# Delta-rule layer on one NeuronCore: six of its causal convolutions move from VectorE to TensorE, and the start is reordered

## The reference, cut to what matters

```python
def conv(x, w):                          # w has 4 taps, shared by all channels
    xp = pad(x, 3 rows of zeros in front)
    return w[0]*xp[:, 0:T] + w[1]*xp[:, 1:T+1] + w[2]*xp[:, 2:T+2] + w[3]*xp[:, 3:T+3]
q = silu(conv(x @ Wq, conv_q)); k = silu(conv(x @ Wk, conv_k)); v = silu(conv(x @ Wv, conv_v))
beta = sigmoid(x @ Wb); q, k = l2norm per head
A = (k*beta) @ k.T ; M = strict_lower(A) + I ; u = M^-1 (v*beta) ; w = M^-1 (k*beta)   # per chunk
# scan over the chunks: u -= w S ; o = q S + lower(q k.T) u ; S += k.T u
o -> per-head RMS norm * onorm_w -> @ Wo
```

## Time and profile before

| what | value |
|---|---|
| profiled execution, device time | 962.78 us |
| its span | 961.0 us (1.8 us lie around it) |
| runs, median | 962.0 us |
| PE, DVE, ACT busy | 86%, 69%, 38% of the span |
| bodies 0 to 8 and their tail | 0 to 702.5 us |
| routed experts and output | 702.5 to 961.0 us |

### The profile page before, as it was taken

One profiled execution on the slowest core, in us unless ns is written; L12 is line 12 of the kernel. 1 busy time (PEld: TensorE's weight loads), 2 busy tenths in 40 slices (PEclk: granted clock), 3 DMA queues, 4 the chain that ended last, 5 costly groups with the idle time before them and its releaser, 6 DMA issues. The chain is left out here.

```text
span 961.0 us, 30663 instructions
## 1 busy us (share of the span) xinstructions
PE 822.5 (86%) x13456; PEld 629.2 (65%) x13456; DVE 661.5 (69%) x1220; ACT 364.8 (38%) x683; POOL 116.7 (12%) x173
## 2 busy tenths in 40 slices
PE   6794779789999999999999787998779999999910
PEld 5683665676777777687687464666566887788800
DVE  2799699799789789879877988787691222222238
ACT  2605334435534644544554451332321222222215
POOL 2000000000000000000000000000002454544345
PEclk9895988999999999999999987998889999999965
DMA  8301004300101021020020020020176999999376
GB/s 307 72 23 47 3 3 168 108 3 25 62 18 39 3 69 27 24 70 23 4 69 24 3 70 23 2 89 2 48 286 220 362 362 346 344 360 358 96 266 278
DMA packets 49632, 113.09 MB, mean 118 GB/s; under 512 B 8688, under 2 KB 8816, under 8 KB 49504
## 3 DMA queue, kind: packets, MB, share of 16 engines
q1 hardware_dynamic: 44384, 100.70, 29.1%
q0 software_dynamic: 5120, 10.49, 4.8%
HBM read 84.34 MB, written 26.84 MB: 116 GB/s over the span
## 5 line engine op out<-in xcount | busy, mean ns | idle before, releaser
L468 PE MATMUL bank<-xnT,wring 128*128 128x256 f32 x768 | 183.6, 396 | 2.1 <-ACTq L681 1.3
L468 PEld LDWEIGHTS bank<-xnT,wring 128*128 128x128 f32 x768 | 149.3, 198 | 24.9 <-ACTq L681 1.5
L587 PE MATMUL bank<-late,ffn_w 128*128 128x256 f32 x480 | 117.3, 394 | 0.0
L1754 DVE TENSOR_TENSOR hid<-ps_g,sg 128x160 f32<-128x160 f32 x32 | 10.4, 324 | 148.5 <-ACT sg L1650 148.5
L942 DVE SCALAR_TENSOR_TENSOR cv<-pre,taps,cv 128x1024 f32<-128x1024 f32 x72 | 92.4, 1283 | 18.1 <-ACTq L707 14.4
L587 PEld LDWEIGHTS bank<-late,ffn_w 128*128 128x128 f32 x480 | 90.8, 195 | 15.2 <-issue 1.1
L1509 POOL MEMSET xgT<- 128x512 f32 x2 | 1.0, 532 | 686.9 <-POOLq L1834 686.9
L1609 PEld LDWEIGHTS ps_g<-xgT,wring 128*128 128x128 f32 x640 | 74.4, 192 | 10.9 <-issue 10.9
L1609 PE MATMUL ps_g<-xgT,wring 128*128 128x128 f32 x640 | 74.8, 275 | 1.3 <-ACT xgT L1640 1.3
L1640 ACT ACTIVATE xgT<-ps_x 128x320 f32<-128x320 f32 x32 | 14.0, 437 | 132.8 <-PE ps_x L1598 132.8
L549 PE MATMUL bank<-wo,o_ch 128*128 128x512 f32 x128 | 60.1, 605 | 0.6 <-DVE o_ch L1086 0.6
(11 more groups left out here) (202 smaller groups left out, 1474.2 us busy)
## 6 DMA issues: line engine op xcount, KB each, us to landing
wring<-in_ffn_W_gate SPq DMA_DIRECT2D x20, 512.0 KB, 7.6
wring<-in_ffn_W_up SPq DMA_DIRECT2D x20, 512.0 KB, 9.6
wring<-in_ffn_W_down SPq DMA_DIRECT2D x20, 512.0 KB, 10.7
x_in<-in_attn_x SPq DMA_DIRECT2D x8, 512.0 KB, 3.7
x_res<-in_attn_x SPq DMA_DIRECT2D x8, 512.0 KB, 4.8
side_rows<-late SPq DMA_DIRECT2D x8, 512.0 KB, 7.0
x_rows<-x SPq DMA_DIRECT2D x8, 512.0 KB, 3.2
h_rows<-h SPq DMA_DIRECT2D x8, 512.0 KB, 4.4
```

The source lines that it names most:

```text
L468: m = te.matmul(bank[:, c * COLS:(c + 1) * COLS], wqkv[:, w, kt, ct * P:(ct + 1) * P], xnT[:, kt, :], start=(kt == 0), stop=(kt == KT - 1))
L587: m = te.matmul(bank[:, c * COLS:(c + 1) * COLS], w[:, kt, ft * P:(ft + 1) * P], hT[:, kt, :], start=(kt == 0), stop=(kt == KT - 1))
```

## The change

Six convolutions are made by matmuls: of k in bodies 1 and 7, of v in bodies 0, 1, 2 and 7. ACT builds 8 matrices of 128 x 128 (the identity times one tap) at the start. For each half (4 of the 8 tiles, 512 columns) PE adds four matmuls, one for each tap, over shifted views of `pre`. The filler letters are C (k) and D (v), each 4 pieces of 2 matmuls and 2 banks. ACT takes the first exponential, and DVE the product, straight from these banks; the bank is released by DVE. DVE's three taps and ACT's second copy go.

In body 0 the k and q convolutions stay on DVE but run in halves; ACT's order is changed so that silu of k starts after three projections; silu and turn of v move ahead of `problems`; the scaling of `wo` goes from DVE's end of body 0 to ACT; the layernorm of step 2 (`first_norm(2)`, X, `take_x(2)`) goes from body 0 and the head of body 1 into the middle of body 1, and one semaphore of the halos becomes three. In bodies 1, 2 and 7 DVE does silu and turn of v right behind residual(1), and ACT takes silu of v behind take_output(0), ahead of the old step's rstd.

```diff
+CONV_K = (1, STEPS - 1)
+CONV_V = (0, 1, 2, STEPS - 1)
-FILLS = {0: ["BGGGGXPPPPPPPPPPPP"],
+FILLS = {0: ["BGGGGDDDDXPPPPPPPPPPPP"],
+         1: ["BCC", "CCD", "DDD", "X", "GPPPP", "G", "G", "G", "PP", "PP", "PP", "", "", "PP", "", "O"],
+         2: ["BXWW", "WWWD", "WWWD", "DDPP", "GPP", "G", "G", "G", "PP", "HPP", "PP", "", "", "PP", "", "EEEEOEEEE"],
+         STEPS - 1: ["BRWWCC", "WWWCC", "WWWD", "DDD", "G", "GFF", "GFF", "GFF", "FF", "H", "", "VVVV", "YYYY", "", "", "EEEEOEEEE"],
...
+        def convolve(s, w, n):
+            section, half = "_CD"[w], n // 2
+            if n == 0:
+                pe.wait_ge(tap_mats, 1)
+                pe.wait_ge(pre_ready[w], s + 1)
+            if n % 2 == 0:
+                ring.wait_free(pe, section, s, half)
+            bank = ring.bank(section, s, half)[:, :].rearrange("p (i t) -> p i t", t=TT)
+            for j in range(2 * (n % 2), 2 * (n % 2) + 2):
+                m = te.matmul(bank, tap_m[:, w - 1, j, :], pre[:, w, 4 * half:4 * half + 4, j:j + TT], start=(j == 0), stop=(j == TAPS - 1))
+            if n % 2 == 1:
+                m.then_inc(ring.full(section, s, half), 1)
...
 ACT: silu_factor
+            if by_matmul(w, s):
+                for half in range(2):
+                    ring.wait_full(act, section, s, half)
+                    link(sc_e.activation(dst[:, 512 * half:512 * half + 512], ring.bank(section, s, half)[:, :], ACT.Exp, scale=-1.0))
+                link(sc_e.activation(dst, dst, ACT.Ln, bias=1.0))
+                sc_e.activation(dst, dst, ACT.Exp, scale=-1.0).then_inc(sig_ready[w], 1)
+                return
...
 ACT: start
-        for n in range(4):
+        for n in range(2):
+            for j in range(TAPS):
+                last = sc_e.activation(tap_m[:, n, j, :], ident[:, :], ACT.Copy, scale=taps[:, n + 1, j:j + 1])
+        last.then_inc(tap_mats, 1)
+        for n in range(3):
             take_projection(0, n)
         silu_factor(0, 1)
+        take_projection(0, 3)
+        rstd(0, 1)
+        silu_factor(0, 0)
         take_projection(0, 4)
-        silu_factor(0, 0)
         take_projection(0, 5)
-        rstd(0, 1)
...
 ACT: body
             take_output(core, 0)
+            if new and by_matmul(2, s):
+                silu_factor(s, 2)
+            if s == 1:
+                take_x(2)
             if last >= 0:
                 rstd(1, last)
                 scale_y(last)
...
 DVE: start
-        conv(0, 1, 0)
+        for half in range(2):
+            conv_half(0, 1, half)
+        halo(1, 0)
         first_moments(1)
-        conv(1, 0, 0)
+        conv_half(1, 0, 0)
         silu_kq(0, 1, 0)
+        conv_half(1, 0, 1)
+        halo(0, 0)
         turn_k(0)
         first_scale(1)
         silu_kq(1, 0, 0)
-        conv_begin(2, 0)
-        conv_end(2, 0)
         for j in range(J):
             masks(0, j)
+        silu_v(0)
+        turn_v(0)
         problems()
...
-        first_norm(2)
...
-            last = v.tensor_scalar(wo[:, ct, :], wo[:, ct, :], onw[:, 0:1], None, ALU.mult)
...
 DVE: body
             if new:
-                conv(0, 1, s)
+                if not by_matmul(1, s):
+                    conv(0, 1, s)
                 conv(1, 0, s)
             next_state(core, 0)
+            if s == 1:
+                first_moments(2)
             if new:
                 silu_kq(0, 1, s)
-                conv_begin(2, s)
+                if s == 1:
+                    first_scale(2)
+                if not by_matmul(2, s):
+                    conv_begin(2, s)
                 silu_kq(1, 0, s)
...
             residual(core, 1)
-            if new:
+            if new and by_matmul(2, s):
+                silu_v(s)
+                turn_v(s)
+            elif new:
                 conv_end(2, s)
```

More of the change, by code:

```diff
@@ L259, in step_part @@
     v_turned = sem("v_turned")
-    halo_done = sem("halo_done")
+    halo_done = [sem(f"halo_done{n}") for n in range(3)]
+    pre_half = sem("pre_half")
+    tap_mats = sem("tap_mats")
     kq_ready = sem("kq_ready")
@@ L300, in quad, with by_matmul @@
         return slice(DK * n, DK * n + DK)
+    def by_matmul(w, s):
+        return (w == 1 and s in CONV_K) or (w == 2 and s in CONV_V)
     block = ctx.enter_context(nc.Block())
@@ L702, in take_projection @@
             bank = ring.bank("P", s, n)[:, :].rearrange("p (i t) -> p i t", t=TT)
[L703 to L704 removed]
+            if by_matmul(w, s):
+                link(sc_e.activation(pre[:, w, 4 * half:4 * half + 4, HALO:], bank, ACT.Copy))
+            else:
+                sc_e.activation(pre[:, w, 4 * half:4 * half + 4, HALO:], bank, ACT.Copy)
+                link(sc_e.activation(cv[:, w, 4 * half:4 * half + 4, :], bank, ACT.Copy, scale=taps[:, w, TAPS - 1:TAPS]))
             release("P", s, n)
+            if s == 0 and half == 0:
+                act.sem_inc(pre_half, 1)
             if half == 1:
@@ L709, in silu_factor @@
         def silu_factor(s, w):
-            act.wait_ge(conv_done[w], s + 1)
             slot = (1, 0, 2)[w]
+            if by_matmul(w, s):
+                section, dst = "_CD"[w], sig[:, slot, :]
+                for half in range(2):
[4 more added lines that the diff above has]
+                return
+            act.wait_ge(conv_done[w], sum(not by_matmul(w, n) for n in range(s + 1)))
             sigmoid(sig[:, slot, :], cv[:, w, :, :].rearrange("p i t -> p (i t)")).then_inc(sig_ready[w], 1)
@@ L813, in _ @@
         key_norms(0)
-        rstd(0, 2)
+        act.wait_ge(small_in, 16 * SMALL)
+        act.wait_ge(weights_in, 16 * 4)
+        for ct in range(CT):
+            last = sc_e.activation(wo[:, ct, :], wo[:, ct, :], ACT.Copy, scale=onw[:, 0:1])
+        last.then_inc(wo_scaled, 1)
         for n in range(BANKS["P"]):
@@ L843, in body @@
                 rstd(2, last)
-            if new:
+            if new and not by_matmul(2, s):
                 silu_factor(s, 2)
@@ L951, in conv_end, with halo, conv_half @@
             dve.sem_inc(conv_done[w], 1)
+            halo(w, s)
+        def halo(w, s):
+            if by_matmul(w, s):
+                ring.wait_full(dve, "_CD"[w], s, 1)
             link(v.tensor_copy(pre[:, w, :, 0:HALO], pre[:, w, :, TT:TT + HALO]))
-            dve.sem_inc(halo_done, 1)
+            dve.sem_inc(halo_done[w], 1)
+        def conv_half(a, w, half):
+            i = slice(4 * half, 4 * half + 4)
+            if half == 0:
+                dve.wait_ge(pre_half, a + 1)
+            else:
+                dve.wait_ge(pre_ready[w], 1)
+            for n in range(TAPS - 1):
+                link(v.scalar_tensor_tensor(out=cv[:, w, i, :], in0=pre[:, w, i, n:n + TT], scalar=taps[:, w, n:n + 1], in1=cv[:, w, i, :], op0=ALU.mult, op1=ALU.add))
+            if half == 1:
+                dve.sem_inc(conv_done[w], 1)
         def silu_kq(a, w, s):
@@ L959, in silu_kq @@
             dve.wait_ge(sig_ready[w], s + 1)
+            if by_matmul(w, s):
+                for half in range(2):
+                    cols, job = slice(512 * half, 512 * half + 512), ("_CD"[w], s, half)
+                    link(v.tensor_tensor(kqs[s % 2][:, 16 * half:16 * half + 16, a, :], ring.bank(*job)[:, :].rearrange("p (g c) -> p g c", c=CH),
+                                         sig[:, slot, cols].rearrange("p (g c) -> p g c", c=CH), ALU.mult))
+                    dve.sem_inc(ring.free(*job), 1)
+                dve.sem_inc(kq_ready, 1)
+                halo(w, s)
+                return
             link(v.tensor_tensor(kqs[s % 2][:, :, a, :], flat(cv[:, w, :, :]).rearrange("p (g c) -> p g c", c=CH), sig[:, slot, :].rearrange("p (g c) -> p g c", c=CH), ALU.mult))
@@ L964, in silu_v @@
             dve.wait_ge(sig_ready[2], s + 1)
+            if by_matmul(2, s):
+                for half in range(2):
+                    job = "D", s, half
+                    link(v.tensor_tensor(flat(cv[:, 2, 4 * half:4 * half + 4, :]), ring.bank(*job)[:, :], sig[:, 2, 512 * half:512 * half + 512], ALU.mult))
+                    dve.sem_inc(ring.free(*job), 1)
+                halo(2, s)
+                return
             link(v.tensor_tensor(flat(cv[:, 2, :, :]), flat(cv[:, 2, :, :]), sig[:, 2, :], ALU.mult))
```

30 lines of the change are left out of this document (15 added, 15 removed).

## The result

The changed kernel took 977.48 us (median of 4 runs, 974.77 to 980.25) against 962.27 for the kernel before on the same chip (958.39 to 968.97): ratio 1.0154, 95% interval 1.0123 to 1.0186. The forecast was 980.5, range 965 to 988. The profiled execution has a span of 978.5 us, 17.5 more than before; the working gave 18.6.

What follows compares the result with a forecast made beforehand. It took PE's list to bound each body's first half and DVE's inverse the second. Terms 0.4 + 7.0 + 3.7 + 7.5 = 18.6 us on the profiled 962.78 gave 981.4, stated as a median of 980.5, range 965 to 988.

Steps and rivals of the forecast that it cites:

- What bounds a body: First half of a body ends with PE's list at the fourth gram, second with DVE's inverse; a body is their sum.
- The price of a record: On PE, 0.43 us per 512-column record; a convolution of 16 records costs 6.9 us, a piece 1.7.
- Body 0: At the start, `problems` moves from 47.83 to 55.6 us; T0 of body 1 comes 0.4 us later, bounds -3 to +3.
- rival B: More matmuls in the gaps may keep PE at 2.4 GHz; body 0's grams gain 2 us; total 976; chance 0.13.
- Body 1: Second solve 9.6 us late, less 2.6 for silu and turn of v: +7.0 us, bounds +2 to +9.
- The 2.5 us charged for the clock: In body 1, PE's list from T0, 15.5 us at full clock, becomes 18.0 for the lower clock after standing.
- Body 2: D's 6.9 us before the second solve delays the fourth mask from 28.7 to 35.0; net +3.7 us, bounds 0 to +5.
- Body 7: C and D add 13.8 us before the grams; second solve moves from 17.4 to 28.9; net +7.5 us, bounds +3 to +9.
- Bodies 3 to 6 and the rest: Bodies 3 to 6 and 8 keep their lists, and the experts move with the last body: no change in length.
- A: PE's slack takes most of the added work: body 1 +3, body 2 0, body 7 +3.5, start -2; total 967; chance 0.16.
- C: DVE is the bound throughout, so the work taken from it comes off the time: total 939; chance 0.10.

Runs made afterwards that it cites:

- rstd_first: Changed kernel, with ACT making the old step's rstd and scale_y ahead of silu of v in bodies 2 and 7: 975.93 us, 1.0143 of the kernel before.
- one_tap: Changed kernel, with only the last tap's matmuls issued in each matmul convolution, three taps left out: 955.07 us, 0.9903 of the kernel before.
- no_body7: Changed kernel, with body 7's convolutions of k and v both back on DVE: 967.21 us, 1.0044 of the kernel before.
- k7_on_dve: Changed kernel, with only k's convolution of body 7 back on DVE, v's staying on PE: 968.45 us, 1.0079 of the kernel before.
- ahead_of_t0: Changed kernel, with two more C pieces and one D of body 1 moved before the first solve: 970.68 us, 1.0110 of the kernel before.
- pad_stream: Kernel before, with 16 small matmuls (32 records) added once at the start of PE's list: 960.17 us, ratio 0.9975.
- start_v_pad: Kernel before, with the start's edits, silu and turn of v ahead of the fourth mask, and 32 small padding records: 949.38 us, ratio 0.9862.

## Why the prediction was right

**What bounds a body.** Right. The first half goes by PE's list to the fourth gram, the second by DVE's inverse: in body 1 the first half grew by 9.4 us (residual(2) at T0 + 42.0, it was 32.6) while the second moved by 0.4.

**The price of a record.** Right: 0.43 from the earlier trace rows; 7.13 us for the 16 of body 0 (predicted 6.9), 5.42 for 12 (5.2) and 3.70 for 8 (3.4).

**Body 0** (+0.4, measured +0.2). `problems` at 55.32, predicted 55.6; DVE's stand 9.22, predicted 9. The grams took 5.3 us, not 6.4, at a granted clock of 1.00 (0.77 from 35 to 42 us before): the part of rival B on body 0 came true, though 1.34 us of it went into a stand.

**Body 1** (+7.0, measured +9.8). Four pieces make up the 2.8 us. The second solve came at T0 + 29.4 instead of 28.3: PPPP began 0.8 us sooner than forecast and took 8.9 us for the 7.0 charged (+1.1). The 7.0 are 32 records at the full clock, and the clock fell to 0.60 behind the stand of 2.44 us. From the solve to the fourth mask 9.07 us passed instead of 8.5, with "issue" stands of 1.65 and 2.28 us on the way, 1.43 and 1.84 before (+0.6). The third, 1.57, and a clock of 0.50 behind it made residual(2) wait 0.83, which the forecast had not. The second half gave +0.4. The 2.5 us charged for the clock lay in the wrong place: at the head, with 0.64 for the first 4.8 us and 1.00 from 91 us on, it cost 1.3 (the solve 1.08 for 0.75, CCD 6.43 for 5.42), and 1.9 more in PPPP, which the sum had at nothing.

**Body 2** (+3.7, measured +2.7). The shift came at T0 + 20.2, forecast for 18.9, after a wait of 4.69 us; it still came before PE's state product, which residual(1) then awaited for 1.06 us more, at T0 + 21.4 (forecast 20.0):

```profile
185.94 0.16 DVE L1188 SCALAR_TENSOR_TENSOR shift<-mv,rs 128x2 f32<-128x2 f32 x1 [4.69 <-ACT rs L694]
187.16 0.45 DVE L1160 STREAM_TRANSPOSE resid<-bank 128x256 f32<-128x256 f32 x1 [1.06 <-PE bank L525]
```

The second solve came at T0 + 25.8 (24.9), and the fourth mask at 34.1 (35.0). The stretch between them took 8.3 us where 10.1 were carried over from before: there the "issue" stands in it were 1.50 and 2.36 us and the last G ran at the low clock (1.93 us), here the stands were 1.08 and 1.77.

**Body 7** (+7.5, measured +10.5). The chain is as predicted: residual(1) behind shift behind rstd, at T0 + 26.5 (predicted 27.7), G0 held by its ring bank, the solve at T0 + 29.3 (28.9). rstd_first confirms it by an edit: without the stand the clock stays at 1.00. Undersized is the stretch from solve to fourth mask: 13.0 us for the 8.9 charged, since the clock behind the 3.46 us stand was 0.50 (the first G took 1.93, not 1.10; FF 3.77, not 1.99) and one stand of 0.86 fell into the solve. ACT's two rows show the release that G0 waits for:

```profile
570.92 0.28 ACT L693 ACTIVATE rs<-mv,eps_ln 128x2 f32<-128x2 f32 x1
...
571.67 1.67 ACT L811 ACTIVATE x<-bank,shift,rs 128x512 f32<-128x512 f32 x2 [0.23 <-DVE shift L1188]
```

The second half took 1.5 less than before, and no edit is tied to that: over the twelve traces it takes 38.4 to 42.1 us. Sum: +4.1 for the stretch, +0.4 for the solve, -1.5.

**Bodies 3 to 6 and the rest** (0, measured -4.3 and -1.4). Missed, and it hid the undersized terms: the three changed bodies and the start give 23.2 us, where 18.6 was forecast. A total that agrees to 1.1 us is here partly luck. By the medians, which differ by 15.2 us, the forecast of 18.5 was 3.3 too high.

**The rivals.** A (PE's slack absorbs) is refuted for the whole by one_tap; for v in body 7 by itself the price is nothing (k7_on_dve). C (DVE is the bound) is refuted by no_body7 and k7_on_dve. B (the clock) is half right: it held for the grams of body 0, and filling the stand ahead of T0 removed the low clock at the head in ahead_of_t0, but the whole edit gave body 1 only 3.9 us, and behind PPPP's stand in body 1 and G0's in body 7 the change created a low clock instead. The Trainium skill, "TensorE: Matmul & The Clock Gate", Part 1, says that the throttled state is the default and activity releases it; the trace agrees in both places, 0.64 behind a stand of 5.03 us and 0.50 behind one of 3.46.

What stays open: how long the clock stays low behind a stand, which differed between ahead_of_t0 and the changed kernel behind the same 3.46 us; what the moved layernorm costs body 1 by itself; and the length of body 7's second half.

## What to carry to other kernels

Split a software-pipelined body at the point where one engine's list hands over to the other's, and charge moved work only to the half in which it lands; busy totals (PE 86%, DVE 69%) say nothing about that. Work is not free because it goes to an engine that idles, and its price hangs on the place: in body 7 the 16 records of v cost nothing, and 16 more of k cost 12.5 us, of which 7.2 is their own time: with them silu of v, ACT's rstd behind it and the bank behind that come later, and PE gets a stand with a low clock behind it. Look for the stands that the new order makes, not only for those that are there, and charge the low clock behind them: in body 1 it cost 1.3 us behind 5.03 us and 1.9 behind 2.44. When a bundle loses, time its parts alone: here the start order (0.9948) and the order of DVE's tail (0.9937) each gain; the matmuls lose (one_tap, no_body7), and so does ACT's silu of v ahead of rstd in body 7 (rstd_first, 4.5 us of the body).

## What was not expected of the hardware

The "issue" stands of PE, 0.2 to 2.7 us, sit almost all inside runs of small 32 x 32 matmul records (in pad_stream one of 2.10 us sits in a run of 512 columns, in start_v_pad one of 2.65), and where they sit depends on the place in PE's stream. In the kernel before, the stand in the same group splits it before its last 22 records in body 3, 21 in body 4 and 20 in body 5. 32 records of padding at the start removed the stands from these bodies (bodies 3 to 6: 307.9 to 302.3 us) and moved or lengthened those of bodies 1 and 2. Body 3 took 77.4 to 75.2 us in four kernels with the same list on PE, so up to 2 us of a body can come and go with nothing changed on PE, which is as much as many edits of this kind are worth.

The traces tie these stands to PE's instructions. The page of the kernel before lists a queue for them:

```profile
q8 instruction: 104, 1.70, 0.7%
```

That is a packet of 16,384 bytes each time. In the twelve traces PE's timelines show 164 "issue" stands behind the first 20 us, and every one ends 2.2 to 3.0 us after the start of such a packet: in body 1 before, packets start at 106.3 and 109.6 us and the stands end at 108.49 and 112.06. Where the stands sit, the packets are some 3.8 us apart, so chance would put about one stand in five there. Between those two stands lie 128 records of PE and as many weight loads. This fits an engine that, in runs of small records, gets through its instructions faster than the next block of them arrives. No run changes how instructions are loaded, so the cause is inferred and not tested.

The clock was low behind shorter stands than the 6 us that the prediction reckoned with. Behind 2.44 us in body 1 it was 0.60 for 3.3 us, behind 3.46 in body 7 0.50 from 572 to 580 us, and behind the same 3.46 in ahead_of_t0 0.57 for 4.0 us and then 1.00.
